# Staging the table blocks of layer 1's s_v scores in a buffer of fixed address, by ScalarE

## The chip, the cores and the metric

The kernel runs on one core of one Trainium2 chip. The metric is the time of one execution on the device in microseconds (us). Five engines run their own streams of instructions side by side and wait for each other by semaphores: TensorE (PE, with its weight loads shown as PEld), VectorE (DVE), ScalarE (ACT), GpSimd (POOL) and SyncE (SP), which issues transfers. The sequencer of an engine, which handles registers, waits and loads of words, appears in the trace as a queue of its own (PEldq, SPq and so on).

## What is computed

A graph of 6250 nodes with 256 features and 100000 edges, sorted by their destination, passes through two layers. Layer 0 is a message MLP with a GRU; layer 1, which the change touches, is attention over 8 heads. Cut to what matters:

```python
def _L1_gnn_ref(x, W_u, b_u, W_v, src, dst):
    s_u = x @ W_u.T + b_u
    s_v = x @ W_v.T
    e = s_u[src] + s_v[dst]
    e = jnp.where(e >= 0, e, 0.2 * e)
    m = jax.ops.segment_max(e, dst, num_segments=n_nodes)
    e_exp = jnp.exp(e - m[dst])
    denom = jax.ops.segment_sum(e_exp, dst, num_segments=n_nodes)
    probs = e_exp / denom[dst]
    xh = x.reshape(n_nodes, head_dim, num_heads)
    out = jax.ops.segment_sum(xh[src] * probs[:, None, :], dst, num_segments=n_nodes)
    return out.reshape(n_nodes, dim)

edge_index = jnp.stack([src, dst])
x = _layernorm(x + _L0_gnn_ref(x, edge_index, edge_attr_64, ...))
x = _layernorm(x + _L1_gnn_ref(x, L1_gnn_W_u, L1_gnn_b_u, L1_gnn_W_v, src, dst))
```

## The kernel before

The program runs in phases: a setup, layer 0 (edges gathered, passed through the MLP and scattered), the nodes' GRU and layer norm, layer 1 over the edges (layer1_phase, from L1228), a merge and the output. The order of the work in layer 1 is written out by hand for each engine; semaphores tie the engines together.

Layer 1 cuts the edges into 784 tiles of 128 edges and these into 49 groups of 16 tiles (NG = 49, GROUP = 16). There are two sets of buffers for gathered features, indices, one-hot matrices and results; group g uses set r = g mod 2. The loop over groups runs 24 times over two bodies, and the last group stands behind the loop. In one group:

- **POOL** gathers, per tile, 128 rows of X1 (256 features and 8 values s_u) into feats[r] with one indirect DMA (L1303). The gather of tile t for group g+2 waits until PE has finished the aggregation of tile t of group g (agg_done), since it overwrites those features.
- **DVE** builds one-hot matrices of the destinations (onehot: which of the 256 nodes in two neighbouring blocks of 128 an edge goes to; same: which edges of a tile share a destination), forms the scores from s_u and s_v (L1430 to L1434), finds the running maxima by scans (L118, L119), subtracts the maximum (L1445) and weights the features four tiles at a time (L1452).
- **PE** gets s_v of every edge as a one-hot product with the table of the nodes' s_v values. The table has a block of 24 columns for every 128 nodes (8 heads in three bf16 parts); a tile reads two neighbouring blocks, and which ones is known only from data. Four block numbers are packed in a word: PE loads the words of a group (L1327), takes them apart in registers, and writes the address of each of the 32 matmuls into a register just ahead of it (L1341). The half groups of 16 matmuls for group g+1 stand in PE's order behind the transposes of the scores (L1354, L1355) and behind the transpose of the maxima into psM (L1361). Then come the 16 aggregation matmuls (L1371) of 264 columns into four PSUM buffers psU in turn; each waits until ACT has emptied its buffer (part_ready).
- **ACT** copies the turned scores from psE (L1380), takes the exponential (L1382), copies the maxima (L1384) and copies each tile's psU to part[r] (L1387), each behind agg_done of that tile.
- **SP** loads the row of local destinations for group g+2 (L1278) and stores part[r] to PT (L1292).

Layer 0 opens its block of engine programs in a stack that is closed at the end of the kernel.

## Time and profile before

| what | us |
| --- | --- |
| time, median of 3 runs | 4833.07 (4831.66 to 4838.84) |
| span of the profiled execution | 4827.7 |
| layer 1, from the first to the last turned copy (48 groups) | 1382.5 |
| of these, PE / DVE / ACT / POOL busy | 743.3 / 505.0 / 359.1 / 759.3 |
| whole span: PE / PEld / DVE / ACT / POOL busy | 3239.8 / 2005.0 / 1819.0 / 1166.8 / 3347.0 |

A row of the trace names an engine, a line of the program, an operation, and its output and inputs by the program's names. Busy time counts neither register instructions nor the issue of transfers. The bracket behind a row of the timeline is the engine's idle time ahead of it and what ended it, as inferred from semaphore events; where one semaphore number is used again by a later phase, the name in the bracket can be that of the earlier use. The granted clock is given as a share of TensorE's full speed.

### The profile page before, as it was taken

The numbers are of one execution on the slowest core, as the hardware profiler recorded it, in microseconds if no ns is written. First come the engines' busy times: TensorE is split into PE (matmuls) and PEld (weight loads), VectorE is DVE, ScalarE is ACT, GpSimd is POOL, SyncE is SP. The second block draws the span as 40 slices with busy tenths as digits, with TensorE's granted clock in tenths as the row PEclk, the third lists the DMA queues.
The fourth block names the chain that finished last, engine by engine and source line by source line (L and its number), as shares of the span: only waits on it lengthen the run. The fifth ranks groups of instructions, "written<-read, shape, count | busy, mean of one in ns | idle before, by whom it ended". The sixth has DMA issues, their size and how long they took to land. (4 is left out here: it accounts for less than half of the span.)

```text
span 4827.7 us, 62259 instructions
## 1 busy us (share of the span) xinstructions
PE 3239.8 (67%) x14137; PEld 2005.0 (42%) x14138; DVE 1819.0 (38%) x3830; ACT 1166.8 (24%) x3229; POOL 3347.0 (69%) x2982
## 2 busy tenths in 40 slices
PE   3568777777887777778877867845554555555536
PEld 1234444444444444444444435533433333333325
DVE  2543333333333333333333338843333433333315
ACT  0222222222222222222222223312222222222212
POOL 4258888888888888888888868975655555555545
PEclk9878988898889888898898889966666666666667
DMA  7686676666667667666667665645564555555553
GB/s 283 187 279 133 124 136 132 124 130 135 128 127 136 131 124 137 134 124 137 134 124 137 133 142 175 205 126 164 171 191 145 184 164 169 168 167 179 171 171 108
DMA packets 570756, 744.54 MB, mean 154 GB/s; under 512 B 181680, under 2 KB 465396, under 8 KB 566884
## 3 DMA queue, kind: packets, MB, share of 16 engines
q0 software_dynamic: 199136, 338.75, 36.5%
q1 hardware_dynamic: 349440, 364.56, 24.6%
q10 hardware_dynamic: 22148, 40.87, 2.7%
q8 instruction: 11, 0.18, 0.0%
q14 instruction: 21, 0.17, 0.0%
HBM read 442.70 MB, written 301.26 MB: 154 GB/s over the span
## 5 line engine op out<-in xcount | busy, mean ns | idle before, releaser
L813 POOL DMA_INDIRECT S<-l_msum,l_sink x784 | 1282.3, 1636 | 247.3 <-issue 213.9
L1303 POOL DMA_INDIRECT l_feats<-X_rows,l_gsrc x784 | 779.9, 995 | 618.1 <-PE l_psU L1371 335.7
L796 POOL DMA_INDIRECT l_ga<-A_rows,l_gsrc x784 | 793.7, 1012 | 259.3 <-issue 166.4
L886 PE MATMUL l_psU<-l_hid,l_same 128*128 128x257 f32 x1568 | 589.8, 462 | 530.7 <-ACT l_hid L922 498.2
L926 ACT COPY l_msum<-l_psU 128x257 f32<-128x257 f32 x784 | 292.6, 373 | 1894.4 <-POOLq L812 1353.5
L859 PE MATMUL l_psC<-l_table,l_onehot 128*128 x4728 | 727.1, 295 | 0.0
L852 PE MATMUL l_psC<-W1cT,l_attrT 64*128 64x256 f32 x1576 | 620.1, 477 | 10.6 <-DMA l_table<-B_rows 10.6
L1371 PE MATMUL l_psU<-l_feats,l_same 128*128 128x264 f32 x1568 | 491.2, 478 | 151.2 <-DVE l_feats L1452 79.7
L859 PEld LDWEIGHTS l_psC<-l_table,l_onehot 128*128 128x128 bf16 x4728 | 425.8, 104 | 365.9 <-issue 304.5
L886 PEld LDWEIGHTS l_psU<-l_hid,l_same 128*128 128x128 f32 x1568 | 268.0, 214 | 666.5 <-ACT l_hid L922 578.2
L1387 ACT COPY l_part<-l_psU 128x264 f32<-128x264 f32 x784 | 296.0, 378 | 747.1 <-DMA B_rows<-su_zeros 347.2
L1371 PEld LDWEIGHTS l_psU<-l_feats,l_same 128*128 128x128 f32 x1568 | 363.7, 239 | 260.8 <-DVE l_feats L1452 82.5
L852 PEld LDWEIGHTS l_psC<-W1cT,l_attrT 64*128 64x128 f32 x1576 | 260.2, 206 | 263.3 <-issue 228.1
L1000 DVE TENSOR_TENSOR l_hidden<-l_psG,bgate 128x256 f32<-128x256 f32 x147 | 62.3, 424 | 797.6 <-PE l_psG L901 672.5
L922 ACT ACTIVATE l_hid<-l_ga 128x256 f32<-128x256 f32 x784 | 331.2, 422 | 0.0
L975 DVE TENSOR_TENSOR l_ga<-l_ga,l_psC 128x256 f32<-128x256 f32 x784 | 307.9, 414 | 40.7 <-issue 12.4
L1361 PE MATMUL l_psM<-ident,l_turned 128*128 128x128 f32 x49 | 22.3, 455 | 420.2 <-DVE l_turned L119 409.7
L118 DVE TENSOR_TENSOR_SCAN l_run<-l_turned 128x128 f32<-128x128 f32 x49 | 20.8, 425 | 732.1 <-ACT l_turned L1380 670.7
L958 DVE TENSOR_SCALAR l_togo<-srcT,spare 128x8 f32 x98 | 27.0, 276 | 715.3 <-POOLq L812 566.9
L1341 PE MATMUL l_psV<-l_table,l_onehot 128*128 x1568 | 245.6, 193 | 70.7 <-issue 34.9
L1452 DVE TENSOR_TENSOR l_feats<-l_feats 128x1024 f32<-128x1024 f32 x196 | 226.9, 1219 | 18.4 <-ACT l_feats L1382 18.0
L1341 PEld LDWEIGHTS l_psV<-l_table,l_onehot 128*128 128x128 bf16 x1568 | 159.2, 103 | 161.9 <-issue 69.7
(303 smaller groups left out, 3615.0 us busy)
## 6 DMA issues: line engine op xcount, KB each, us to landing
PT<-l_part SPq DMA_DIRECT2D x49, 2176.0 KB
l_srcb<-src_rows SPq DMA_DIRECT2D x99, 512.0 KB
S<-su_zeros ACTq DMA_DIRECT2D x24, 1156.5 KB
l_locb<-loc_rows SPq DMA_DIRECT2D x51, 512.0 KB
l_locb<-loc_rows SPq DMA_DIRECT2D x99, 256.0 KB
nd_sums<-S SPq DMA_DIRECT2D x196, 128.5 KB
l_attr<-in_edge_attr SPq DMA_DIRECT2D x98, 256.0 KB
GH_rows<-l_hidden SPq DMA_DIRECT2D x49, 384.0 KB
```

The source lines that it names most:

```text
L796: pool.indirect_dma_start(ga[:, s, :], None, D["A"], bass.IndirectOffsetOnAxis(ap=gsrc[h][:, j % HALF:j % HALF + 1], axis=0)).then_inc(gat ...
L813: pool.indirect_dma_start(D[f"S{j % NTAB}"], bass.IndirectOffsetOnAxis(ap=sink[j // HALF][:, j % HALF:j % HALF + 1], axis=0), msum[:, j % ...
L852: nc.tensor.matmul(pc(j), attrT[j // 4 % 2][side, j % 4 // 2 * P:(j % 4 // 2 + 1) * P], K["W1cT"][side, :], start=True, stop=False)
L859: t = nc.tensor.matmul(pc(j), onehot[j // HALF % 2][:, w, j % HALF, :], flat(table[:, bass.ds(blocks[j % 4] + w, 1), n * H:(n + 1) * H]), ...
L886: nc.tensor.matmul(psU[j % 2][:, 0:UW], same[j // HALF][:, j % HALF, :], hid[:, j % RING, :], start=True, stop=True).then_inc(agg_done, 1)
L922: nc.scalar.activation(hid[:, j % RING, 0:H], ga[:, j % SLOTS, :], ACT.Relu).then_inc(hid_ready, 1)
L926: nc.scalar.copy(msum[:, j % RING, :], psU[j % 2][:, 0:UW]).then_inc(msum_ready, 1)
L975: nc.vector.tensor_tensor(ga[:, s, :], ga[:, s, :], pc(j), ALU.add).then_inc(pre_ready, 1)
L1303: pool.indirect_dma_start(feats[r][:, t, :], None, D["X1"], bass.IndirectOffsetOnAxis(ap=gsrc[r][:, t:t + 1], axis=0)).then_inc(gathered[r ...
L1341: i = nc.tensor.matmul(psV[:, t * NSPLIT * NH:(t + 1) * NSPLIT * NH], onehot[r][:, w, t, :], flat(table[:, bass.ds(blocks[t % PACK] + w, 1 ...
L1371: nc.tensor.matmul(psU[t % 4][:, 0:XW], same[r][:, t, :], feats[r][:, t, :], start=True, stop=True).then_inc(agg_done, 1)
L1387: nc.scalar.copy(part[r][:, t, 0:XW], psU[t % 4][:, 0:XW]).then_inc(part_ready, 1)
```

## The change

Two new buffers window[r], of 16 tiles by 48 columns in bf16, take the two table blocks that each tile of a group needs. ACT fills them: it loads a word of block numbers every fourth tile, takes it apart in registers, and copies 128 x 48 values from the table into window[r][:, t, :]. The tiles of the first two groups (32 copies) are staged ahead of ACT's loop; those of group g+2 stand one by one behind the copy of part of tile t of group g. PE's matmuls for s_v read window at an address that is fixed when the program is built, and wait once per group for window_ready; PE's load of words and its registers for the table are gone. Beside that the number of buffer sets has a name (SETS = 2), SP no longer loads rows of destinations for groups that don't exist, DVE doesn't copy the last group's indices ahead, POOL's first gathers wait for their own set of indices alone, and layer 0's block is closed and its semaphores are cleared before the nodes phase.

```diff
@@ layer 0
-        block = st.enter_context(nc.Block())
+        phase = ExitStack()
+        block = phase.enter_context(nc.Block())
@@ end of layer 0
+        phase.close()
+        m.clear_sems()
@@ layer 1, buffers and semaphores
+        window = [m.sb(f"window{r}", [P, GROUP, WIN * NSPLIT * NH], BF16) for r in range(SETS)]
+        window_ready = m.sem("window_ready")
@@ layer 1, SP
-            groups(sp, body)
+            groups(sp, body, NG - SETS)
+            for g in range(NG - SETS, NG):
+                store(g, g % SETS)
@@ layer 1, POOL
-            pool.wait_ge(index_ready, 2)
-            for r in range(2):
+            for r in range(SETS):
+                pool.wait_ge(index_ready, r + 1)
                 for t in range(GROUP):
                     gather(r, t)
@@ layer 1, PE
-            def dst_scores(g, r, words, half):
+            def dst_scores(g, r, half):
                 if half == 0:
                     pe.wait_ge(onehot_ready, g + 1)
+                    pe.wait_ge(window_ready, g + 1)
                 for t in range(half * HALF, (half + 1) * HALF):
-                    if t % PACK == 0:
-                        blocks = unpack(nc, words[t // PACK])
                     for w in range(WIN):
                         i = nc.tensor.matmul(psV[:, t * NSPLIT * NH:(t + 1) * NSPLIT * NH], onehot[r][:, w, t, :],
-                                             flat(table[:, bass.ds(blocks[t % PACK] + w, 1), :]),
+                                             window[r][:, t, w * NSPLIT * NH:(w + 1) * NSPLIT * NH],
                                              start=(w == 0), stop=(w == WIN - 1))
-            pe.wait_ge(table_ready, 1)
-            words = load_blocks(0)
-            dst_scores(0, 0, words, 0)
-            dst_scores(0, 0, words, 1)
+            dst_scores(0, 0, 0)
+            dst_scores(0, 0, 1)
@@ layer 1, ACT
+            def stage_window(g, r, t, blocks):
+                i = nc.scalar.copy(window[r][:, t, :], flat(table[:, bass.ds(blocks[t % PACK], WIN), :]))
+                if t == GROUP - 1:
+                    i.then_inc(window_ready, 1)
+
+            act.wait_ge(table_ready, 1)
+            for g in range(2):
+                for t in range(GROUP):
+                    if t % PACK == 0:
+                        blocks = window_blocks(nc, act, K, (g * GROUP + t) // PACK)
+                    stage_window(g, g, t, blocks)
@@ layer 1, ACT, in the loop body
                 for t in range(GROUP):
                     act.wait_ge(agg_done, g * GROUP + (t + 1))
                     nc.scalar.copy(part[r][:, t, 0:XW], psU[t % 4][:, 0:XW]).then_inc(part_ready, 1)
+                    if not last:
+                        if t % PACK == 0:
+                            blocks = window_blocks(nc, act, K, g * (GROUP // PACK) + (2 * GROUP + t) // PACK)
+                        stage_window(g + 2, (r + 2) % SETS, t, blocks)
@@ layer 1, DVE
-                stage_index(g + 2, r)
+                if not last:
+                    stage_index(g + SETS, r)
```

PE, in the loop of layer 1, from the transposes of the scores to that of the maxima, before (the pair of L1341, an instruction that writes the address and the matmul, stands sixteen times):

```order
L1354 MATMUL l_psE<-ident,l_score 128x128
L1355 MATMUL l_psE<-ident,l_start 128x128
L1327 ISA
L1327 TENSOR_LOAD blocks
L1336 REGISTER_ALU
L1341 ISA
L1341 MATMUL l_psV<-l_table,l_onehot 128x24
...
L1361 MATMUL l_psM<-ident,l_turned 128x128
```

and after:

```order
L1355 MATMUL l_psE<-ident,l_score 128x128
L1356 MATMUL l_psE<-ident,l_start 128x128
L1340 REGISTER_ALU
L1344 MATMUL l_psV<-l_window,l_onehot 128x24 x16
L1361 MATMUL l_psM<-ident,l_turned 128x128
```

The load of words and the sixteen address instructions are gone from between the matmuls; the second half, behind L1361, changes in the same way. PE's whole program shrinks from 892 to 700 rows.

ACT, in the same loop, from the turned copy to the first tiles' copies of part, before:

```order
L1380 COPY l_turned<-l_psE 128x256
L1382 ACTIVATE l_feats<-l_below 128x16x8
L1383 ISA
L1384 COPY l_part<-l_psM 128x16x8
L1386 ISA
L1387 COPY l_part<-l_psU 128x264
L1386 REGISTER_ALU
```

and after (one window copy with its address instruction follows every copy of part, the load of a word every fourth one):

```order
L1393 COPY l_turned<-l_psE 128x256
L1395 ACTIVATE l_feats<-l_below 128x16x8
L1396 ISA
L1397 COPY l_part<-l_psM 128x16x8
L1399 ISA
L1400 COPY l_part<-l_psU 128x264
L150 ISA
L150 TENSOR_LOAD blocks
L150 ISA x2
L1380 ISA
L1380 COPY l_window<-l_table 128x48
```

What stood on PE's side of the aggregation now stands between two copies of part. ACT's whole program grows from 337 to 506 rows.

## Rows read from the trace of the kernel before

**Rows 1.** Page's first line; busy us by stretch: PE, PEld, DVE, ACT, POOL, clock

```profile
span 4827.7 us, 62259 instructions
...
3210.50:4593.00 1382.50, 743.32 (x3216) 532.73 (x3216) 505.02 (x719) 359.07 (x936) 759.31 (x765) 0.66 0.55 169
...
4578.60:4593.00 14.40, 11.79 (x51) 9.08 (x51) 9.12 (x13) 6.78 (x20) 0.00 (x0) 0.72 0.42 141
```

**Rows 2.** Timeline of ACT, one group: start, us, operation, idle before it

```profile
4027.24 0.37 ACT L1380 COPY l_turned<-l_psE 128x256 f32<-128x256 f32 x1
...
4033.85 0.38 ACT L1387 COPY l_part<-l_psU 128x264 f32<-128x264 f32 x1 [2.44 <-PE l_psU L1371]
...
4037.37 2.60 ACT L1387 COPY l_part<-l_psU 128x264 f32<-128x264 f32 x6 [0.50 <-issue]
4041.80 0.38 ACT L1387 COPY l_part<-l_psU 128x264 f32<-128x264 f32 x1 [1.83 <-PE l_psU L1371]
...
4055.25 0.38 ACT L1387 COPY l_part<-l_psU 128x264 f32<-128x264 f32 x1 [1.74 <-DMA B_rows<-su_zeros]
4056.71 0.37 ACT L1380 COPY l_turned<-l_psE 128x256 f32<-128x256 f32 x1 [1.08 <-DMA blocks<-block_words]
```

**Rows 3.** Timeline of POOL, the same group, first and last of 16 gathers

```profile
4034.64 0.96 POOL L1303 DMA_INDIRECT l_feats<-X_rows,l_gsrc  x1 [6.89 <-PE l_psU L1371]
...
4056.03 0.94 POOL L1303 DMA_INDIRECT l_feats<-X_rows,l_gsrc  x1 [1.17 <-DMA B_rows<-su_zeros]
```

**Rows 4.** Timeline of PE, the same group

```profile
4045.84 2.01 PE L1341 MATMUL l_psV<-l_table,l_onehot 128*128 x16
4058.05 0.47 PE L1361 MATMUL l_psM<-ident,l_turned 128*128 128x128 f32 x1 [10.20 <-DVE l_turned L119]
```

**Rows 5.** Timeline of ACT, the last group but one

```profile
4586.94 6.16 ACT L1387 COPY l_part<-l_psU 128x264 f32<-128x264 f32 x14 [0.47 <-PE l_psU L1371]
```

**Rows 6.** Timeline of ACT, group 13

```profile
3591.65 0.38 ACT L1387 COPY l_part<-l_psU 128x264 f32<-128x264 f32 x1 [2.44 <-PE l_psU L1371]
...
3598.68 0.38 ACT L1387 COPY l_part<-l_psU 128x264 f32<-128x264 f32 x1 [0.78 <-PE l_psU L1371]
3600.83 0.38 ACT L1387 COPY l_part<-l_psU 128x264 f32<-128x264 f32 x1 [1.77 <-DMA B_rows<-su_zeros]
...
3603.69 0.38 ACT L1387 COPY l_part<-l_psU 128x264 f32<-128x264 f32 x1 [1.04 <-DMA B_rows<-su_zeros]
```

**Rows 7.** Timeline of PE and DVE, the end of group 13

```profile
3609.85 0.45 PE L1361 MATMUL l_psM<-ident,l_turned 128*128 128x128 f32 x1
...
3620.04 0.18 PE L1341 MATMUL l_psV<-l_table,l_onehot 128*128 x1 [1.11 <-issue]
...
3626.47 0.29 DVE L1445 TENSOR_TENSOR l_below<-l_score,l_psM 128x128 f32<-128x128 f32 x1 [16.42 <-DMA loc_rows<-su_locpad]
```

**Rows 8.** Register instructions and loads, SP's and PE's queues, ns min/median/max

```profile
L1278 SPq FUSED_REGOPS  x48: 3/60/724, 3195.1 to 4576.4; - x48
...
L1341 PEldq FUSED_REGOPS  x1568: 2/91/1397, 3197.7 to 4582.5; - x196
...
L1327 PEldq TENSOR_LOAD <-blocks x49: 328/331/1076, 3197.2 to 4565.0; - x49
```

**Rows 9.** Groups by line and shape, layer 1: xcount | busy us, mean ns

```profile
L1384 ACT COPY l_part<-l_psM 128x128 f32<-128x128 f32 x42 | 10.4, 247 | 0.0
```

**Rows 10.** Timeline of PE and DVE at the start of layer 1

```profile
3198.31 5.14 PE L1341 MATMUL l_psV<-l_table,l_onehot 128*128 x30 [0.15 <-issue]
...
3208.59 0.49 DVE L1430 TENSOR_REDUCE l_score<-l_psV 128x128 f32<-128x384 f32 x1
```

**Rows 11.** Waits in layer 1: us in total, times, longest

```profile
ACT l_part L1387 <- DMA B_rows<-su_zeros: 347.2, 129, 4.6
...
DVE l_below L1445 <- DMA loc_rows<-su_locpad: 54.3, 9, 16.4
```

**Rows 12.** The clear of semaphores behind the setup, ns

```profile
L98 POOLq EVENT_SEMAPHORE_RANGE_CLEAR  x1: 270/270/270, 289.1 to 289.1; - x1
```

More of the change, by code:

```diff
@@ L1239, in layer1_phase @@
         table = m.sb("table", [P, NB + 1, NSPLIT * NH], BF16)
-        same = [m.sb(f"same{r}", [P, GROUP, P]) for r in range(2)]
-        part = [m.sb(f"part{r}", [P, GROUP, PW]) for r in range(2)]
+        same = [m.sb(f"same{r}", [P, GROUP, P]) for r in range(SETS)]
+        part = [m.sb(f"part{r}", [P, GROUP, PW]) for r in range(SETS)]
         score = m.sb("score", [P, GROUP, NH])
@@ L1266, in groups @@
         def groups(engine, body, count=NG):
-            with engine.Fori(0, count // 2) as u:
-                for r in range(2):
-                    body(u * 2 + r, r, u, False)
-            if count % 2:
-                body(count - 1, 0, count // 2, True)
+            with engine.Fori(0, count // SETS) as u:
+                for r in range(SETS):
+                    body(u * SETS + r, r, u, False)
+            for r in range(count % SETS):
+                body(count // SETS * SETS + r, r, count // SETS, True)
         @block.sync
@@ L1281, in _, with store @@
             sp.dma_start(svf[:, :, :], D["sv"].rearrange("(b p) h -> p b h", p=P)).then_inc(table_in, 16)
-            for r in range(2):
+            for r in range(SETS):
                 sp.sem_inc(stored[r], 16)
                 dst_rows(r, slice(r * GROUP, (r + 1) * GROUP))
-            def body(g, r, u, last):
-                sp.wait_ge(same_ready, g + 1)
-                dst_rows(r, bass.ds(g * GROUP + 2 * GROUP, GROUP))
+            def store(g, r):
                 sp.wait_ge(part_ready, g * GROUP + GROUP)
@@ L1293, in body @@
                              part[r][:, :, :]).then_inc(stored[r], 16)
-            groups(sp, body)
-            for r in range(2):
-                sp.wait_ge(stored[r], 16 * ((NG + 1 - r) // 2) + 16)
-                sp.wait_ge(dst_in[r], 16 * ((NG + 1 - r) // 2 + 1))
+            def body(g, r, u, last):
+                sp.wait_ge(same_ready, g + 1)
+                dst_rows(r, bass.ds(g * GROUP + SETS * GROUP, GROUP))
+                store(g, r)
+            groups(sp, body, NG - SETS)
+            for g in range(NG - SETS, NG):
+                store(g, g % SETS)
+            for r in range(SETS):
+                sp.wait_ge(stored[r], 16 * len(range(r, NG, SETS)) + 16)
+                sp.wait_ge(dst_in[r], 16 * len(range(r, NG, SETS)))
         @block.gpsimd
@@ L1408, in compare @@
                                         ALU.is_equal).then_inc(same_ready, 1)
-            stage_index(0, 0)
-            stage_index(1, 1)
+            for r in range(SETS):
+                stage_index(r, r)
             find_node(0, 0, 0)
```

39 lines of the change are left out of this document (17 added, 22 removed).

## The prediction

> **What bounds the kernel now.** I first read the busy table by stretch. Layer 1's 48 steps between turned score tiles run from 3210.5 to 4593.0 us, 1382.5 us or 28.8 us a group, and no engine is full there: POOL is busy 759 us, PE 743, DVE 505, ACT 359 [rows 1]; the whole span is 4827.7. So a chain bounds it. The timeline of one ordinary group shows the chain on ACT. The copy of the turned scores is at 4027.24 in the group before and at 4056.71 here: 29.5 us. The first copy out of psU is at 4033.85. Nine more follow, the last six in 2.60 us, that is one per 0.44; the first four came one per 0.88, at the lower TensorE clock. Then the copies fall apart: from 4041.80 to 4055.25 there are five intervals, 2.69 us each on average [rows 2]. A DMA on B_rows, named there as the releaser, is a stale name of a reused semaphore: the copy waits for agg_done, which is PE's.
>
> PE's own timeline says that its work was handed out long before: the sixteen s_v matmuls of the next group's first half start by 4045.84 and PE has no further start until 4058.05 [rows 4]. The start of a matmul is recorded, its completion is not, and the completions come late. What runs all that time is POOL's train of sixteen gathers, one per 1.25 us (0.95 busy, 0.30 between), from 4034.64 to 4056.03 [rows 3]. In the last but one group there is no gather left to issue, POOL is busy 0.00, and fourteen copies take 6.16 us: no stall [rows 1, 5]. Bare register instructions on two queues show the same thing from another side: on SP one that normally takes 0.060 took up to 0.724, on PE one of 0.091 up to 1.397, both near multiples of 0.7 [rows 8]. I read this so: while gathers are issued back to back, whatever PE and SP have to retire passes one by one, at about 0.7 us each, after some slack is used up. Of the 49 groups 41 show such a tail; six (every seventh) and the last two don't. In all ACT waits 347.2 us under that stale name before copies of part, the largest idle time on the chain [rows 11].
>
> **What queued s_v instructions do to the tail.** In group 13 the scores came late, so PE's queue stood before the s_v matmuls while the tail ran. There the last three copies are 2.86 us apart in all, 1.43 each [rows 6], against 2.69 in the ordinary group, where register instructions and matmuls of s_v had been issued behind. A second sight: in that same group the s_v matmuls themselves, issued with the train on, take from 3609.85 to 3620.04 instead of 2.6 us, and DVE's subtraction behind psM waits 16.42 us [rows 7]. Over layer 1 nine such waits sum to 54.3 us [rows 11].
>
> **The change part by part.**
>
> PE loses, per half group, 16 register instructions before its 16 s_v matmuls, and per group one table load of 0.331 [rows 8]. At full pace that is worth nothing: the second half ends before the first weighted tile, and in the first half PE waits for the scan anyway. Its worth lies in the tail. The register instructions are a third of what s_v puts into PE's queue (16 of 16 registers, 16 weight loads, 16 matmuls). The tail's five intervals cost 13.45 us, at group 13's 1.43 they would cost 7.15; the difference is 6.3, a third of it 2.1. There is a cap: POOL's train needs 15 x 1.25 + 0.95 = 19.7 us from 4034.64, so it ends no sooner than 4054.3, and psM's transpose stands behind sixteen s_v matmuls that don't get through before; now it is at 4058.05. From the train's end to the transpose I leave 1 us: the cap is 2.7. I take 1.8 a group: 41 x 1.8 = -74. The ends are 0 (the pace of 0.7 belongs to matmuls and weight loads alone) and -111. The nine late subtractions: a third of 54.3, -18 (0 to -27).
>
> ACT gains per tile one register instruction and one copy of 128x48, and per four tiles a load with its registers. No such copy is in the trace. From above it costs what the 128x264 copy does, 0.378; through the two rows (0.247 for 128 columns, 0.378 for 264) a line gives 0.17 at 48 [rows 2, 9]. I take 0.22, near the smaller, whose size it is near. With 0.33 + 0.2 of load per four tiles, a tile costs ACT about 0.44 + 0.22 + 0.06 + 0.13 = 0.85 us in place of 0.44 (0.7 to 0.95). Who waits for it: PE, through the four psU buffers. In the ordinary group tiles 4 to 9 slow from 0.44 to 0.85, but they only fill the slack sooner or later; the tail's gaps of 1.7 us and more hide the rest. Behind the last tile one window copy stands before the turn of the scores. ACT is the late one there in about half of the groups: 24 x 0.25 = +6 (0 to +12). In the last but one group nothing covers it: about 12 x 0.4 = +5 (3 to 8). The six groups without a tail are counted in that half.
>
> The Trainium skill speaks against such copies: Perfetto Trace Analysis, Optimizing Scalar/DVE Operations, gives a ScalarE operation on SBUF a fixed overhead of some 93 ns, with a profiled latency about twice that, and advises grouping. By it the copy would last near 0.23 us, an estimate from that page, and the sum would not move; no row here shows a copy that small.
>
> Start: ACT must stage sixteen tiles before the first s_v matmul, about 7 us, and sixteen more before it turns anything. Now PE starts its 32 at 3197.8 and is done by 3203.5, and DVE takes them at 3208.6 because the gathers land only then, so 5 us are hidden [rows 10]: +2 for the rest. Against that, psM's long wait behind the opening train loses a third too, -4. Together -2 (-4 to +8). The clearing of semaphores behind layer 0 adds a barrier and a clear of 0.270 [rows 12]: +0.6, twice that at most. DVE's changes (index staging, buffer numbers) and SP's two missing row loads at the end lie beside other work: 0.
>
> Sum: -74 - 18 + 6 + 5 - 2 + 0.6 = -82. The profiled span is 4827.7, the median of the three runs 4833.07, 5.4 more: 4745 and 4751 us.
>
> **The rivals.**
>
> A. The tail does not care for registers. For: POOL's rate alone seems to set it, and the matmuls and weight loads that remain are two thirds of the queue. Then only costs are left, 6 + 5 + 2 + 0.6: 4847, up to 4865 with the upper prices. Chance 0.22.
>
> B. The slower pace itself avoids the tail. The tail sets in behind a burst at 0.44 a tile, never while tiles come at 0.88, as if slack were used up by the burst [rows 2, 6]. With 0.85 a tile the sixteen are done 13 us after the first, and the cap of the train decides: 2.7 x 41 with all of the rest, 4833 - 111 - 27 + 13 = 4708. If the s_v matmuls get through too, the train of 20 us plus a few bounds the group, 23 us: 41 x 6 less, about 4590. Chance 0.20, of it 0.06 for the latter.
>
> C. The other side, one mechanism: the tail sets in at a fixed time after the train has begun, not at a fixed count. Then ACT's 0.85 lets about 2 tiles fewer through before it (2.2 us at 0.85 instead of 0.44), and each costs 2.1, midway between 1.43 and 2.69, instead of 0.44: +3.3 a group, 41 x 3.3 = +135, 4968. It decides from a tile on ACT above 0.44. Against it: the first late copy comes 8.0 us after the first one in the ordinary group, in group 13 7.0 us after it [rows 2, 6]. Chance 0.04.
>
> D. The gain is 0.3 us a group and the costs eat it: 4833 within 10. Chance 0.10.
>
> E. ACT's loop grows by some 130 instructions, and each of its 24 returns might have to wait for instructions. No row shows such a pause on any engine; priced by the longest wait for a word that PE had, 1.076 us [rows 8], it is 26 us: 4777. Chance 0.02. A rule of the Trainium skill stands behind this one: Runtime: NRT & Kernel Launch, Instruction fetch mechanics, lets a taken branch to a page outside the current window stall for its fetch.
>
> **How the numbers follow.** Main case 0.42, A 0.22, B 0.20, C 0.04, D 0.10, E 0.02. What a measurement of this kernel can tell is about 0.2%, 10 us. Faster: main, B, E: 0.64. Same: D 0.10 and a bit of A: 0.12. Slower: 0.24. The main case's own range is 4705 to 4810; the one for 8 in 10 reaches over A and the first half of B, and leaves out B's far end and C: 4650 to 4870.
>
> **What the changed profile would show.** In an ordinary group the copies of part come at 0.7 to 0.9 us through the first tiles; window copies near 0.22; the tail's intervals are shorter than 2.69, near 2.2; from turn to turn 27 to 28 us. If the tail's intervals stay at 2.7, A holds. If there is no tail, B. If the tail begins two tiles earlier, C. The subtraction behind psM should wait less than 54 us in all. I would be wrong above all if the 0.7 us steps are not shared between register instructions and matmuls.

## The result and the profile after

The changed kernel takes 4799.44 us (median of 7 runs) against 4829.71 of before (7 runs): a ratio of 0.9938, interval 0.9923 to 0.9952, or 30 us less. The forecast was 82 us less. The sign was right, the size was not, and the experiments show that the reason was not either.

The page of after begins:

```profile
span 4794.3 us, 63031 instructions
...
PE 3109.8 (65%) x14137; PEld 1915.3 (40%) x14138; DVE 1822.6 (38%) x3829; ACT 1256.6 (26%) x4030; POOL 3360.8 (70%) x2982
```

PE is busy 130 us less, ACT 90 us more, and POOL 14 us more (12 of them in layer 1's gathers, 779.9 to 792.0). The 33.4 us between the two spans can be laid out by events of the timelines (in us):

| stretch | before | after | change |
| --- | --- | --- | --- |
| start to the first gather of layer 1 | 3184.2 | 3189.5 | +5.3 |
| first gather to the first copy of part | 46.3 | 54.6 | +8.3 |
| first copy of part to the last turned copy | 1362.5 | 1314.8 | -47.7 |
| last turned copy to the end | 234.7 | 235.4 | +0.7 |

The gain lies in the loop; the start of layer 1 gives some of it back. The first row is not the change's: a second profile of the changed kernel (e13) has 3182.8 there, and kernels without the clear of semaphores have up to 3194.9 (e15). The timeline of ACT shows an ordinary group of after (start, duration, operation, count, idle before it), the one that answers to [rows 2]:

```profile
4015.49 0.37 ACT L1393 COPY l_turned<-l_psE 128x256 f32<-128x256 f32 x1 [1.00 <-DMA block_words<-su_word_i]
...
4022.10 0.38 ACT L1400 COPY l_part<-l_psU 128x264 f32<-128x264 f32 x1 [2.44 <-PE l_psU L1371]
4022.91 0.23 ACT L1380 COPY l_window<-l_table 128x48 bf16 x1 [0.42 <-issue]
...
4025.03 0.38 ACT L1400 COPY l_part<-l_psU 128x264 f32<-128x264 f32 x1
4025.82 0.23 ACT L1380 COPY l_window<-l_table 128x48 bf16 x1 [0.41 <-issue]
4025.96 0.37 ACT L1400 COPY l_part<-l_psU 128x264 f32<-128x264 f32 x1
...
4026.36 0.38 ACT L1400 COPY l_part<-l_psU 128x264 f32<-128x264 f32 x1
4026.64 0.24 ACT L1380 COPY l_window<-l_table 128x48 bf16 x1
4026.77 0.39 ACT L1400 COPY l_part<-l_psU 128x264 f32<-128x264 f32 x1
...
4033.01 0.38 ACT L1400 COPY l_part<-l_psU 128x264 f32<-128x264 f32 x1 [2.28 <-issue]
...
4037.29 0.38 ACT L1400 COPY l_part<-l_psU 128x264 f32<-128x264 f32 x1 [3.77 <-DMA S<-su_zeros]
4038.71 0.23 ACT L1380 COPY l_window<-l_table 128x48 bf16 x1 [1.04 <-issue]
4041.53 0.38 ACT L1400 COPY l_part<-l_psU 128x264 f32<-128x264 f32 x1 [2.60 <-DMA S<-su_zeros]
...
4041.94 0.38 ACT L1400 COPY l_part<-l_psU 128x264 f32<-128x264 f32 x1
...
4042.34 0.39 ACT L1400 COPY l_part<-l_psU 128x264 f32<-128x264 f32 x1
...
4042.75 0.39 ACT L1393 COPY l_turned<-l_psE 128x256 f32<-128x256 f32 x1
```

Two things differ from [rows 2]. A copy of part and a window copy together take 0.41 us (4026.36 to 4026.77), since the second begins while the first is ending; such a pair costs ACT no more than the single copy every 0.44 did. Only the steps in which a word of block numbers is loaded are longer (4025.03 to 4025.96, 0.93). And the tail is of another shape: its intervals are longer, up to 4.28 us (4033.01 to 4037.29, against 3.51 in [rows 2]'s group), but there are fewer of them, and then three copies and the turned copy come in one burst, 0.41 apart. The group takes 27.3 us, not 29.5. POOL in the same group, to be read against [rows 3]:

```profile
4022.89 0.96 POOL L1314 DMA_INDIRECT l_feats<-X_rows,l_gsrc  x1 [8.50 <-PE l_psU L1371]
...
4038.07 0.95 POOL L1314 DMA_INDIRECT l_feats<-X_rows,l_gsrc  x1 [0.35 <-issue]
4042.31 0.95 POOL L1314 DMA_INDIRECT l_feats<-X_rows,l_gsrc  x1 [3.30 <-DMA S<-su_zeros]
4043.56 0.95 POOL L1314 DMA_INDIRECT l_feats<-X_rows,l_gsrc  x1 [0.31 <-issue]
4044.82 2.24 POOL L1314 DMA_INDIRECT l_feats<-X_rows,l_gsrc  x1 [0.30 <-issue]
```

After thirteen gathers POOL has to wait 3.30 us for PE, and the burst on ACT begins at the end of this pause (4041.53, the next gather at 4042.31). I read it so: PE's finished work passes when no gather is under way. The turned copy (4042.75) is 2.07 us ahead of the last gather's start (4044.82); before it was 0.68 us behind it, 4056.71 against 4056.03. PE's timeline has the new wait of the change:

```profile
4034.09 0.27 PE L1356 MATMUL l_psE<-ident,l_start 128*128 128x128 f32 x1
4043.01 0.58 PE L1344 MATMUL l_psV<-l_window,l_onehot 128*128 128x24 bf16 x16 [8.64 <-ACT l_window L1380]
4044.11 0.48 PE L1361 MATMUL l_psM<-ident,l_turned 128*128 128x128 f32 x1 [0.52 <-DVE l_turned L119]
```

The sixteen s_v matmuls, which in [rows 4] start in the middle of the tail, now wait for window_ready, which ACT's last window copy gives, and then take 0.58 us in place of 2.01. The instructions that take the block words apart, now on ACT, show the steps of [rows 8] there (ns, min/median/max):

```profile
L150 ACTq SEQ_ASSERT  x200: 4/18/727, 3203.2 to 4557.4; - x100
```

### The profile page after: what moved, and what is told of

It is laid out like the page before. It is cut to its first block and busy times, and to the rows that moved or that the text cites. A ratio compares the mean times of both kernels' runs of the same rounds, so it can differ in the third digit from the quotient of the medians.

```text
span 4794.3 us, 63031 instructions
## 1 busy us (share of the span) xinstructions
PE 3109.8 (65%) x14137; PEld 1915.3 (40%) x14138; DVE 1822.6 (38%) x3829; ACT 1256.6 (26%) x4030; POOL 3360.8 (70%) x2982
## 5 line engine op out<-in xcount | busy, mean ns | idle before, releaser
L1314 POOL DMA_INDIRECT l_feats<-X_rows,l_gsrc x784 | 792.0, 1010 | 569.8 <-PE l_psU L1371 264.2
L1371 PE MATMUL l_psU<-l_feats,l_same 128*128 128x264 f32 x1568 | 527.5, 497 | 339.9 <-issue 174.3
L976 DVE TENSOR_TENSOR l_ga<-l_ga,l_psC 128x256 f32<-128x256 f32 x784 | 308.0, 414 | 43.6 <-issue 13.4
L1344 PE MATMUL l_psV<-l_window,l_onehot 128*128 128x24 bf16 x1568 | 59.7, 182 | 310.9 <-ACT l_window L1380 170.9
L1380 ACT COPY l_window<-l_table 128x48 bf16 x800 | 187.4, 235 | 159.1 <-issue 133.9
L902 PE MATMUL l_psG<-WhhT,l_xgT 128*128 128x256 f32 x588 | 195.9, 418 | 0.0
```

The source lines that it names most:

```text
L976: nc.vector.tensor_tensor(ga[:, s, :], ga[:, s, :], pc(j), ALU.add).then_inc(pre_ready, 1)
L1314: pool.indirect_dma_start(feats[r][:, t, :], None, D["X1"], bass.IndirectOffsetOnAxis(ap=gsrc[r][:, t:t + 1], axis=0)).then_inc(gathered[r ...
L1371: nc.tensor.matmul(psU[t % 4][:, 0:XW], same[r][:, t, :], feats[r][:, t, :], start=True, stop=True).then_inc(agg_done, 1)
```

## One table for the loop

The same four pieces were taken from the timelines of every kernel: the 28 groups from 1 to 46 that are neither a fast one (5, 12, 19, 26, 33 and 40, the six every seventh that have no tail before) nor one of the two behind it, mean of each piece in us. The last column is the start of the copy of part of tile 15 less the start of gather 15.

| kernel | turned copy to first copy of part | gather 0 to gather 15 | gather 15 to next turned copy | group | copy 15 - gather 15 |
| --- | --- | --- | --- | --- | --- |
| before | 6.67 | 21.17 | +0.92 | 29.54 | -0.93 |
| after | 6.62 | 21.57 | -0.97 | 28.00 | -2.31 |
| after, a second profile | 6.62 | 21.42 | -0.47 | 28.35 | -1.84 |
| registers only | 6.72 | 19.57 | +1.49 | 28.55 | -1.65 |
| gate only | 6.61 | 20.10 | +1.59 | 29.08 | -1.39 |
| registers and gate | 6.81 | 19.52 | +2.00 | 29.11 | -1.32 |
| staging only | 6.75 | 21.63 | -0.94 | 28.22 | -2.21 |
| staging, tiles 0 to 7 | 6.66 | 21.38 | -0.84 | 27.97 | -2.27 |
| staging, tiles 8 to 15 | 6.62 | 21.73 | -0.58 | 28.55 | -1.78 |
| hold at tile 12, on before | 7.71 | 21.60 | -4.02 | 26.62 | -6.18 |
| hold at tile 12, on after | 6.63 | 22.75 | -3.32 | 26.88 | -4.44 |
| hold at tile 8, on before | 11.03 | 22.55 | -10.85 | 26.53 | -13.31 |

(From the first copy of part to gather 0 it is 0.78 us everywhere but with the holds: 1.33, 0.83 and 3.79.) A gather train without a pause is 15 x 1.25 = 18.8 us. There are two ways to a shorter group: fewer pauses in the train, or a turn that comes earlier against the train's end. The kernels without staging go the first way, those with staging or a hold the second.

Each row is one profiled execution. That of gate only is 11 us above its kernel's median time, that of registers only 8 below, that of registers and gate 9 above, and the two profiles of the changed kernel differ by 0.35 us a group: differences below some 0.4 us a group say nothing here.

One fixed cost shows in all of these kernels, and neither the prediction nor the experiments touched it. Once per turn of ACT's loop, ahead of the turned copy of every even group, stands an ACT_TABLE_LOAD of 1.28 us. In the changed kernel's timeline of ACT:

```profile
3349.32 1.28 ACT L1393 ACT_TABLE_LOAD   x1
3350.62 0.37 ACT L1393 COPY l_turned<-l_psE 128x256 f32<-128x256 f32 x1
```

From the copy of part of tile 15 to the turned copy it takes 1.82 to 1.84 us in all fourteen of the 28 groups that end so, and as little as 0.40 in the others; by that the load alone holds up the turn, by up to 1.4 us. The groups that end so are 1.4 us longer than the others in this profile (28.69 against 27.30) and 0.35 longer in the second one. Over 23 such turns the load may cost up to some 30 us, an estimate from these rows and as much as the change gains. Before, nine of the fourteen turns stand like that (1.71 to 1.75). No run here moved it.

## The experiments

**Which part of the change gains.** Theory R is the prediction's: PE's lighter queue. Theory G: the wait for window_ready, which holds the s_v matmuls back. Four kernels on one chip, before 4829.35 us.

*Registers only* (e1), from the changed kernel:

```diff
                     pe.wait_ge(onehot_ready, g + 1)
-                    pe.wait_ge(window_ready, g + 1)
+                    pe.wait_ge(window_ready, 2)
...
                     nc.scalar.copy(part[r][:, t, 0:XW], psU[t % 4][:, 0:XW]).then_inc(part_ready, 1)
-                    if not last:
-                        if t % PACK == 0:
-                            blocks = window_blocks(nc, act, K, g * (GROUP // PACK) + (2 * GROUP + t) // PACK)
-                        stage_window(g + 2, (r + 2) % SETS, t, blocks)
```

> The changed kernel without ACT's copies inside the loop: the windows of the first two groups are staged ahead of the loop and all later groups read these (so s_v is stale from group 2 on). PE has the fixed addresses, no table load, no address registers and no wait for a fresh window; ACT has the work of before. Theory R (PE's lighter queue shortens the tail): the gain of the changed kernel is here in full and ACT's tax is gone, so it is faster than the changed kernel: 4740 to 4785 us against 4829.7 of before. Theory G (the gain comes from the new wait for window_ready, which keeps the s_v matmuls out of PE's queue until the last copy of part): nothing is gained here, and the dearer start (8 to 14 us) is left: 4835 to 4845.

Measured: 4807.25 us, ratio 0.9960 (0.9941 to 0.9979), 22 us less. It carries the dear start (54.7 us from the first gather to the first copy of part), so its loop gained more: 1322.3 us from the first copy of part to the last turned copy, 1362.5 before. It is below theory G's 4835 and above the range of theory R, and not faster than the changed kernel (0.9938; the intervals overlap): no tax fell away with the staging.

*Gate only* (e2), from the kernel before with the clear of e5:

```diff
                     pe.wait_ge(onehot_ready, g + 1)
+                    if gated:
+                        pe.wait_ge(tiles_out, g)
...
                     nc.scalar.copy(part[r][:, t, 0:XW], psU[t % 4][:, 0:XW]).then_inc(part_ready, 1)
+                act.sem_inc(tiles_out, 1)
+            act.sem_inc(tiles_out, 1)
```

> The kernel before, with the clear behind layer 0 (the added semaphore needs it) and one wait more: PE's first half of s_v matmuls for group g+1 waits until ACT has passed its last copy of part of group g-1, which is where window_ready stands in the changed kernel. Table reads, load of words and address registers stay on PE; ACT stages nothing. Theory G: the tail gives back what it does in the changed kernel, 40 to 60 us, and there is no dearer start: 4770 to 4790. Theory R: no gain, 4825 to 4850, since 32 matmuls and 32 registers now stand behind the train instead of beside it.

Measured: 4815.65 us, ratio 0.9973 (0.9956 to 0.9990), 14 us less. Neither range holds. The wait does something, but a quarter to a third of what G asked.

*Staging only* (e3), from the kernel before:

```diff
                     nc.scalar.copy(part[r][:, t, 0:XW], psU[t % 4][:, 0:XW]).then_inc(part_ready, 1)
+                    if not last:
+                        if t % PACK == 0:
+                            blocks = window_blocks(nc, act, K, g * (GROUP // PACK) + (2 * GROUP + t) // PACK)
+                        nc.scalar.copy(window[r][:, t, :], flat(table[:, bass.ds(blocks[t % PACK], WIN), :]))
```

> The kernel before with ACT's copies of table blocks in the loop, as in the changed kernel, but into a buffer that nobody reads; PE reads the table as before. This is ACT's tax alone, and the slower pace of the copies of part alone. Theory T (ACT's own register instructions pass at 0.7 us while gathers are issued, and its copies of part stand behind them): slower, +10 to +50 us. Rival B of the prediction (the slower pace itself avoids the tail): faster by 20 us or more. Neither: 4830 within 10.

Measured: 4793.65 us, ratio 0.9928 (0.9903 to 0.9953), 36 us less. This is pure added work whose output nobody reads, and it gains as much as the whole change. In the table it has the changed kernel's pattern: long train, early turn.

*Registers and gate* (e4): the edit of e1 with the wait of e2 added.

> As the first one (fixed addresses on PE, stale windows, no staging in the loop), with the wait of the second one. It is the changed kernel without ACT's tax. If R and G both hold and add up it is the fastest of the four, 4740 to 4775. If G alone holds it equals the gate alone plus the dearer start, 4780 to 4800. If R alone holds it equals the first one within 10 us.

Measured: 4801.62 us, ratio 0.9947 (0.9927 to 0.9968), which cannot be told from e1. That is what was expected if R alone held.

**The parts around it.** Four more on the same chip, before 4829.14 us.

*Clear only* (e5): the kernel before with `phase.close()` and `m.clear_sems()` behind layer 0.

> The kernel before with layer 0's block closed and its semaphores cleared, nothing else. The prediction priced it at 0.6 us. In the profiled execution layer 1 begins 5.3 us later after than before, of which layer 0 itself is 3.3. If the clear is 0.6 us: 4830 within 5. If it carries the 5.3 us: 4835.

Measured: 4832.63 us, ratio 1.0007 (0.9991 to 1.0023). Its layer 1 begins at 3186.1 us. No cost clear of the noise: 3.5 us, with an interval from 4 less to 11 more.

*Direct start* (e6), from the changed kernel:

```diff
-                    pe.wait_ge(window_ready, g + 1)
+                    pe.wait_ge(window_ready, g)
...
-            for g in range(2):
+            for g in range(1, 2):
                 for t in range(GROUP):
...
                     stage_window(g, g, t, blocks)
...
-            dst_scores(0, 0, 0)
-            dst_scores(0, 0, 1)
+            pe.wait_ge(table_ready, 1)
+            pe.wait_ge(onehot_ready, 1)
+            for t in range(GROUP):
+                if t % PACK == 0:
+                    blocks = window_blocks(nc, pe, K, t // PACK)
...
+                                         flat(table[:, bass.ds(blocks[t % PACK] + w, 1), :]),
```

> The changed kernel, but PE reads the table itself for group 0, as before, and ACT stages only group 1 ahead of the loop. In the changed kernel the first copy of part came 54.6 us behind the first gather against 46.3 before, since PE's first s_v matmuls were issued 19 us into the opening train and were through only behind it. If that is the cause, the first turned copy comes some 20 us earlier again and the time falls by 8 to 14 us: 4786 to 4792. If the start costs nothing that counts: 4799.

Measured: 4793.52 us, ratio 0.9924 (0.9909 to 0.9940), 6 us below the changed kernel's median, with intervals that overlap. The first turned copy still comes 46.2 us behind the first gather (48.0 in the changed kernel, 26.3 before), so the cause that I had named, PE's late start, is not enough. The timelines of PE and DVE say what happens:

```profile
3208.90 1.23 PE L1356 MATMUL l_psV<-l_table,l_onehot 128*128 x7 [0.63 <-issue]
3210.85 0.18 PE L1356 MATMUL l_psV<-l_table,l_onehot 128*128 x1 [0.71 <-issue]
...
3232.63 0.56 DVE L1456 TENSOR_REDUCE l_score<-l_psV 128x128 f32<-128x384 f32 x1 [20.66 <-remote]
```

PE begins its s_v matmuls 14.4 us behind the first gather, hardly later than before (13.6), but idle steps of 0.63 to 0.71 us appear between its batches, and DVE gets the scores 21.8 us after the last start, when the train is over. Before, 30 matmuls went in one piece and DVE had them at 3208.59 [rows 10]. What differs is ACT, which runs sixteen window copies at the same time, and PE, which loads four words where it loaded one set. Which of the two uses up the slack was not tried; staging only (e3), which has neither at the start, has a start of 26.2 us.

*Quiet* (e7): the window copies of the changed kernel moved out of the copies of part, eight behind the turned copy and eight behind the copy of the maxima. *Quiet with gate* (e8): the same, with the wait of e2.

```diff
                 nc.scalar.copy(turned[:, 0:2 * P], psE[:, 0:2 * P]).then_inc(scores_kept, 1)
+                if not last:
+                    stage_half(g, r, 0)
...
                 nc.scalar.copy(part[r][:, :, XW:PW], psM[:, 0:P].rearrange("p (t h) -> p t h", h=NH)).then_inc(max_kept, 1)
+                if not last:
+                    stage_half(g, r, 1)
```

> The changed kernel with ACT's sixteen window copies of a group moved out of the copies of part: eight behind the turned copy, eight behind the copy of the maxima, where no gather is being issued and ACT waits. window_ready is then given a group ahead, so it holds PE back no more. Theory R: ACT's tax goes, PE's gain stays: 4770 to 4785. Theory G: the s_v matmuls are again in PE's queue during the train, and the gain goes: 4830 to 4845.

> As the quiet one, with the wait for ACT's last copy of part put back on PE. Theory G: the gain is back and ACT's tax is gone: 4765 to 4785. Theory R: as the quiet one within 10 us.

Measured: 4820.81 us, 0.9981 (0.9966 to 0.9996), and 4825.25 us, 0.9990 (0.9976 to 1.0004). Neither range of e7 holds, and e8 is within 10 us of it, as theory R had it. Most of the gain is gone with the place of the copies, and that has a plain cause: in this timeline of ACT (e7) the second eight delay the first copy of part, which comes 7.27 us behind the turned copy here and 8.2 on average over the 28 groups, not 6.6. Behind that the group is much that of registers only: the gathers take 20.3 us and the turned copy comes 1.1 us behind them.

```profile
4082.33 0.37 ACT L1399 COPY l_turned<-l_psE 128x256 f32<-128x256 f32 x1 [3.93 <-DMA block_words<-su_word_i]
...
4087.49 0.78 ACT L1380 COPY l_window<-l_table 128x48 bf16 x4 [0.33 <-issue]
4088.82 0.77 ACT L1380 COPY l_window<-l_table 128x48 bf16 x4 [0.56 <-issue]
4089.60 0.38 ACT L1410 COPY l_part<-l_psU 128x264 f32<-128x264 f32 x1
```

**Why added work gains.** Theory P: the slower pace of ACT ahead of the tail spares slack (the prediction's rival B). Theory W: what the staging does is to make POOL wait in the middle of its train, and while POOL issues nothing, PE's queue runs empty. Four kernels were to tell this: the staging of e3 behind tiles 0 to 7 only, behind tiles 8 to 15 only, and POOL's wait put in directly, on the kernel before and on the changed one:

```diff
                 for t in range(GROUP):
-                    pool.wait_ge(agg_done, g * GROUP + (t + 1))
+                    pool.wait_ge(agg_done, g * GROUP + (t + 1 if t < 12 else GROUP))
```

> The kernel before with one number changed: POOL's gathers of tiles 12 to 15 wait until PE has finished all sixteen tiles of the group, not just their own. Theory W (what the staging gives comes from POOL having to wait in the middle of its train: while it issues nothing PE's queue runs empty, and the transposes for the next turn are through before the last gathers instead of behind them): in ordinary groups the turned copy moves from 0.92 us behind the last gather's start to 1 us or more ahead of it, the train stays near 21.5, the group falls from 29.5 to 28 or below, 4780 to 4795 in all. Theory P (ACT's slower pace at the start of the aggregation gives it): the train grows by what POOL waits, 4830 to 4870.

> The staging alone (the kernel before, copies into a buffer that nobody reads), but only behind tiles 0 to 7: half of the copies, all of them before the copies of part fall apart. Theory P (pace): most of the 36 us of the full staging is here, 4795 to 4805. Theory W: the late intervals are not longer, POOL waits no earlier, and nothing is gained: 4822 to 4835.

> The staging alone, only behind tiles 8 to 15, where the copies of part are 1.4 to 4.2 us apart: no change of pace before. Theory W: the gain of the full staging, 4790 to 4800, with the turned copy about 1 us ahead of the last gather's start. Theory P: 4825 to 4835.

> The changed kernel with the same hold in POOL as the first of these. Theory W: staging already makes POOL wait at tiles 11 to 13, so the hold adds little or nothing: 4785 to 4805. If the two add up, 4760 to 4775.

These four fell on another chip, where the kernel before takes 4584.72 us (29 runs), 245 us less. Measured, as ratios: 1.0001 (0.9992 to 1.0010), 0.9998 (0.9990 to 1.0007), 0.9991 (0.9982 to 1.0000), and for the hold on the changed kernel 0.9962 (0.9948 to 0.9975). They don't tell the theories apart, for there is nothing to explain there: in the traces of these four, inside a group, the copies of part are no more than 0.98 us apart (a single 1.2 in the first group of two of them). ACT's timeline of e9:

```profile
3412.85 0.38 ACT L1387 COPY l_part<-l_psU 128x264 f32<-128x264 f32 x1 [0.50 <-PE l_psU L1371]
3413.66 6.16 ACT L1387 COPY l_part<-l_psU 128x264 f32<-128x264 f32 x14 [0.43 <-PE l_psU L1371]
```

Fourteen copies take 6.16 us beside a train that runs without a pause, and PE's address registers, 2/91/1397 ns in [rows 8], are here

```profile
L1341 PEldq FUSED_REGOPS  x1568: 55/78/147, 3174.6 to 4330.7; - x196
```

So the 0.7 us steps are no property of the program. Where they are missing, a group takes 24.1 us on average (e9, groups 1 to 46; 28.9 in the kernel before where they are), and 23.7 in the changed kernel with the hold, which gains 18 us in all. The piece that differs there is the head: the first copy of part comes 6.8 us behind the turned copy, not 7.5; that it is the cause was not tried apart, and the changed kernel without the hold was not run on this chip.

The open runs were made again on chips with the tail. The halves of the staging differ from e3 in one line, `if not last and t >= HALF:` for the late one and `t < HALF` for the early one. *The changed kernel again and the late half* (e13, e14), before 4836.82 us:

> The changed kernel as it is. The last four runs fell on another chip, on which the kernel before takes 4584.7 us and its copies of part never come more than 0.93 us apart: the tail is not there. If this run falls on that chip it tells what the change is worth without a tail: theory R gives nothing there (0 within 10 us), since the hold, which the changed kernel had with it there, costs nothing either; a gain of 10 to 20 us would be the shorter stretch of PE between the turn and the first tile (6.8 in place of 7.5 us). If it falls on the first chip: 4799 within 5.

> The staging alone behind tiles 8 to 15, once more. On the chip with the tail: theory W (POOL made to wait in the middle of its train) 4790 to 4800, with the turned copy about 1 us ahead of the last gather's start; theory P (pace ahead of the tail) 4825 to 4835. On the chip without it: within 0.2% of before, as it was.

Measured: 4794.37 us, 0.9917 (0.9897 to 0.9938), and 4806.4 us, 0.9949 (0.9931 to 0.9967). So the change was worth 42 us on this chip, 30 in the first measurement. The late half lies between the ranges of the two theories. *The early half and the holds* (e15 to e17), before 4832.81 us:

> The staging alone behind tiles 0 to 7, once more, for a chip with the tail. The late half alone gave 4806.4 against 4836.8 of before, 30 of the 36 us of the full staging. Theory W: the early half gives nothing, 4820 to 4840. Theory P: 4800 to 4815.

> The kernel before with POOL's gathers of tiles 12 to 15 held until PE has finished all sixteen tiles, once more, for a chip with the tail; no staging, no change on PE or ACT. Theory W: in ordinary groups the turned copy moves from 0.92 us behind the last gather's start to 1 us or more ahead of it and the train is 21 to 22 us; 4780 to 4800. Theory P: the train grows by POOL's wait, 4830 to 4870.

> The changed kernel with the same hold, once more, for a chip with the tail. PE's queue is lighter, so with the hold it should drain sooner than in the run ahead. Theory W: POOL waits in the middle anyway here, 4770 to 4800.

Measured: the early half 4792.48 us, 0.9907 (0.9886 to 0.9929); the hold on the kernel before 4735.8 us, 0.9793 (0.9774 to 0.9812); the hold on the changed kernel 4755.98 us, 0.9839 (0.9822 to 0.9857). One number in POOL's wait, with nothing changed on ACT or PE, gains 97 us, three times what the change does. Theory P has no place for that, and it had forecast a loss. W had the direction, but its ranges (4780 to 4800, and 4770 to 4800 for the hold on the changed kernel) asked too little. The two don't add up: with the hold in place the change costs 20 us (4755.98 against 4735.8), 7 of them at the start of layer 1. W's forecast that the early half gives nothing was wrong, though, since the early half gives all of the 36 us. P's own mechanism is not seen either. ACT's pace hardly changes: the first eight intervals sum to 5.4 us there, 5.2 before. And no slack is spared: the very first interval aside, the first one above 1.25 us follows copy 8.25 on average, counted from 0, and 9.25 before. The tail sets in 5.6 us behind the first copy of part, 5.9 before (and 5.9 in the changed kernel), so with a tile less through POOL catches up with PE sooner. The mean pauses ahead of gathers 12 to 15 are 1.3, 0.3, 0.2 and 0.2 us there, in e3 1.6, 0.6, 0.1 and 0.1, and before 0.0, 0.1, 1.4 and 0.8. The late half gets to the same place by longer intervals (0.3, 1.4, 1.0, 0.2). Either way the pause moves from the last two gathers to the middle. That the pause makes the gain is an argument from this table; no run took the pause away and left the staging. Here is the hold on the kernel before (e16) around group 3, first the timeline of POOL with the four held gathers of group 2, then that of ACT:

```profile
3311.97 1.09 POOL L1303 DMA_INDIRECT l_feats<-X_rows,l_gsrc  x1 [3.11 <-DMA B_rows<-su_zeros]
3313.37 2.40 POOL L1303 DMA_INDIRECT l_feats<-X_rows,l_gsrc  x1 [0.30 <-issue]
3316.07 1.50 POOL L1303 DMA_INDIRECT l_feats<-X_rows,l_gsrc  x1 [0.30 <-issue]
3317.88 1.97 POOL L1303 DMA_INDIRECT l_feats<-X_rows,l_gsrc  x1 [0.30 <-issue]
...
3335.57 0.95 POOL L1303 DMA_INDIRECT l_feats<-X_rows,l_gsrc  x1 [0.30 <-issue]
```

```profile
3311.47 0.38 ACT L1380 COPY l_turned<-l_psE 128x256 f32<-128x256 f32 x1
...
3331.66 0.38 ACT L1387 COPY l_part<-l_psU 128x264 f32<-128x264 f32 x1 [1.05 <-DMA B_rows<-su_zeros]
...
3335.88 0.37 ACT L1380 COPY l_turned<-l_psE 128x256 f32<-128x256 f32 x1 [2.52 <-DMA blocks<-block_words]
```

The held gathers run beside the head of the next group (3311.47 to 3318.09), where before a gather was rare. Group 3 itself takes 24.4 us, and POOL makes no pause in it: its gather of tile 12 starts at 3335.57, when all sixteen tiles have long been copied. Such groups are 7 of the 28, and the shorter ones: 25.5 us against 27.0, and from the first to the last copy of part 14.9 against 17.4. So what the hold shows is that gathers issued beside the aggregation draw out its tail (from the first to the last copy of part 21.0 us before, 16.7 here, 13.0 with the hold at tile 8 below), and that taking them from there shortens the group; a pause inside the train is not needed for it.

*Hold at tile 8* (e18), on the kernel before, before 4830.91 us:

> The kernel before with POOL's hold at tile 8 in place of 12: eight gathers run beside the aggregation, eight behind it, beside the head of the next group. Theory W in its simple form: POOL is quiet as soon as gather 7 is out, 9.9 us behind the train's start, the rest of PE's queue drains at once, and the group is bounded by the two halves of the train, some 23 us: 4650 to 4690. If the gathers that now run beside the next group's head slow the transposes and s_v there (in the run with the hold at 12 the first copy of part already comes 7.7 us behind the turn, 6.7 before), the gain is given back: 4735 to 4800.

Measured: 4720.35 us, 0.9763 (0.9738 to 0.9788), the fastest on a chip with the tail, 110 us below before. The simple form of W asked for 4650 to 4690 and asked too much; the other expectation, that the gathers pushed into the head cost there, has the right mechanism and set its range too high. ACT in groups 3 and 4:

```profile
3305.76 0.31 ACT L1382 ACTIVATE l_feats<-l_below 128x128 f32<-128x128 f32 x1 [3.33 <-DVE l_below L1445]
...
3327.80 0.37 ACT L1380 COPY l_turned<-l_psE 128x256 f32<-128x256 f32 x1 [3.25 <-DMA blocks<-block_words]
3339.64 0.31 ACT L1382 ACTIVATE l_feats<-l_below 128x128 f32<-128x128 f32 x1 [11.47 <-DVE l_below L1445]
```

In 13 of the 28 groups the exponential waits for the subtraction and this for psM's transpose, whose start is recorded at 3329.15 and which is seen only when POOL's eight gathers are out (3336.16 the last). By the table the turn comes 11.8 us earlier against the last gather than before. The head takes back 4.4 of these (11.0 us from turn to first copy of part), the later first gather 3.0 and the longer train 1.4, which leaves 3.0.

## Why the prediction was right or wrong

**What bounds the kernel.** Right, as far as it went: layer 1's time on these chips is the tail beside POOL's train, and what PE and SP have to retire passes in steps of 0.7 us. It holds for ACT too, which the prediction did not reckon with (727 ns for an instruction of 18). What it left out is that the chain goes through POOL's own waits. The last two gathers of the ordinary group have 1.98 and 1.17 us of idle ahead of them; the prediction reckoned with a train that nothing holds up.

**PE's lighter queue, -74.** This is the step that failed: 41 x 1.8, a microsecond off the tail counted as one off the group, and that beside the staging too. The tail itself did shorten. By the table, from the first to the last copy of part it is 21.0 us before (0.78 + 21.17 - 0.93) and 18.7 with registers only (0.78 + 19.57 - 1.65), 2.3 less. But the turned copy then comes 3.1 us behind the last copy of part (1.49 + 1.65), not 1.9, and the group gains 1.0 (29.54 to 28.55). Beside the staging the lighter queue is worth nothing measurable: 28.22 without it, 28.00 and 28.35 with it. I read it as two effects that work through the same pause and don't add up; which of PE's work takes the time between the last copy and the turn was not tried. What the term was scaled from, 1.43 us an interval in group 13 without s_v instructions in the queue, did not carry over: the last five intervals sum to 13.4 us before, 11.5 with registers only and 12.3 with the gate, which keeps the first half's s_v matmuls out of the tail, and not to 7.15. The gate is worth 14 us in all.

**ACT's staging, +11.** The sign was wrong: staging alone gains 36 us (e3). The price of a tile on ACT, 0.85 us, failed because it added durations: copy and window copy overlap and take 0.41 together, and over the first eight intervals the pace is 0.69 us in place of 0.65. The Trainium skill's fixed overhead (Perfetto Trace Analysis, Optimizing Scalar/DVE Operations) fits the duration, 0.23 us. The same section says that a profiled latency overlaps the next instruction with its write-acknowledgement half, which the prediction passed over; the trace agrees, 0.38 and 0.23 us taking 0.41. Rival B named ACT as a possible source of gain, with 4708; its mechanism, slack spared by a slower pace, is not what the runs show, since the pace is hardly slower and the tail sets in a tile sooner.

**The late subtractions, -18.** In the twelve groups behind the fast ones, the first copy of part came later than the usual 6.6 us behind the turn by 55 us in all before, and by 26 and 23 in the two profiles after, somewhat more of a gain than the forecast's far end of 27. The reason was wrong: staging alone has 29, the registers alone 64.

**The start, -2.** Measured +8.3, just above the upper price of the prediction. The cover that it named, DVE waiting for gathers until 3208.6, was gone: PE's first s_v start was at 3208.4, 19 us into the train, and DVE had the scores at 3235.5. The timeline of PE and DVE, to be read against [rows 10]:

```profile
3208.41 1.01 PE L1344 MATMUL l_psV<-l_window,l_onehot 128*128 128x24 bf16 x32 [27.28 <-issue]
...
3235.51 0.56 DVE L1448 TENSOR_REDUCE l_score<-l_psV 128x128 f32<-128x384 f32 x1 [21.55 <-remote]
```

The matmuls last 1.01 us and their end is seen 26 us later, behind the train. A step that is moved under a train is not merely moved. But e6, which moved it back, won 1.8 us of the 21.7 by which the first turned copy is late, so the late start is not the whole cause.

**End of group, last group but one, clear, DVE and SP: +12.** In the last group but one, 16.1 us in place of 14.4, +1.7 (forecast +5). The six fast groups and the last but one together took 111.1 us before and 122.8 after; the prediction had counted them in a half of 0.25 us each. No cost of the clear stands clear of the noise.

**The rivals.** A (4847 to 4865) and D are out by the measured 30 us. C's first half came about: the tail sets in at the same time behind the first copy of part, 5.9 us, and a tile earlier. Its consequence was the opposite of what was forecast. E's pauses are not seen on ACT: at 20 of the loop's 23 returns the next instruction (3349.32 above) starts 0.02 to 0.04 us behind the end of the last window copy. The measured time lies inside the range; the main case's own range of 4705 to 4810 holds it only at its edge, and the way to it is not the one that was given.

## What to carry to other kernels

Where one engine's train of transfers slows what the others have to retire, look how many of the transfers must run beside that work: holding back the last of them by one number (97 and 110 us here) can be worth more than taking instructions off the slowed engine. Test each part of a change alone, the ones priced as a cost too: here the part that was added work made the gain, and two parts worth 22 and 36 us alone made 30 to 42 together. A microsecond off one stretch of a chain is one off the whole only if the next step is ready for it. Before pricing many small instructions, look whether their durations overlap.

## What the hardware showed unexpectedly

The steps of 0.7 us belong to the chip on which a run falls, and so do 245 us of 4830: by the traces of the kernel before and of e9 some 200 of these lie between layer 1's first copy of part and its last turned copy, 14 between its first gather and that copy, and 34 outside layer 1. On three chips the kernel before took 4829 to 4837 us with copies of part up to 5.0 us apart; on a fourth it took 4584.7 us, and in the traces from there none is above 0.98 (one 1.2 at the start), and register instructions that reached 1397 ns took at most 147. There the two halves of the staging and the hold on the kernel before change nothing (ratios 0.9991 to 1.0001). Why the chips differ no run here shows, nor what exactly the steps are; that a kernel tuned against the tail is tuned for some chips only is what the numbers say.
